# Attention in rounds of two key steps, and eight staging buffers ahead of it

## The reference, cut to what matters

```python
qkv = x @ w_qkv                      # q, k, v; 16 heads; q1, q2 and k1, k2 are halves of a head
a1 = softmax(q1 @ k1.T * scale)      # 1024 x 1024 for every batch and head
a2 = softmax(q2 @ k2.T * scale)
out = (a1 - lam * a2) @ v
out_n = out / rms(out) * norm_w * (1.0 - LAMBDA_INIT)
x = x + reshape(out_n) @ wo          # the reshape mixes heads and rows
x = x + bitlinear(relu(bitlinear(layernorm(x)) + gate * low_rank) ** 2)
```

## Time and profile before

| | |
|---|---|
| time, median of 3 runs | 4335.0 us (4332.88 to 4342.35) |
| time of the profiled execution | 4334.89 us |
| its span | 4333.2 us |
| mean granted TensorE clock | 0.986 |
| busy: PE, DVE, ACT | 4148.5, 3193.5, 2870.7 us |
| first projection matmul | 31.7 us after the start |
| first score of pair 0 | 152.9 us after the start |
| last value products | 3097.9 us |

### The profile page before, as it was taken

The page is one execution under the profiler, slowest core; times in us unless marked ns, Lnnn a source line. Parts: engine busy times, 40 slices in busy tenths (PEclk is TensorE's granted clock), DMA queues, the critical chain, the costliest instruction groups (busy, mean ns, idle before and its releaser), DMA issues.

```text
span 4333.2 us, 57624 instructions
## 1 busy us (share of the span) xinstructions
PE 4148.5 (96%) x22152; PEld 2097.1 (48%) x22152; DVE 3193.5 (74%) x3014; ACT 2870.7 (66%) x3572; POOL 2.0 (0%) x14
## 2 busy tenths in 40 slices
PE   5799999999999999999999999999769999999999
PEld 4333333333333333333333333333257777777777
DVE  4688888888888888888888888899664555555554
ACT  2588878878887887888788788899643333333333
POOL 0000000000000000000000000000000000000000
PEclk9899999999999999999999999999879999999999
DMA  4534433434443443343344334433020101101010
GB/s 159 129 94 97 93 98 90 115 84 94 99 94 96 93 113 83 93 102 93 94 93 114 83 83 108 102 68 68 23 71 20 39 20 39 33 27 39 20 39 20
DMA packets 225843, 338.25 MB, mean 78 GB/s; under 512 B 86704, under 2 KB 107184, under 8 KB 225008
## 3 DMA queue, kind: packets, MB, share of 16 engines
q1 hardware_dynamic: 225520, 333.88, 31.9%
HBM read 180.72 MB, written 150.99 MB: 77 GB/s over the span
## 4 chain that ended last, share of the span: by engine, by line
PE 89%; DVE 3%; DMA 3%; ACT 2%; issue 1%; SPq 1%; DVEq 0%; ACTq 0%
PE ps L534 22%; PE ps L509 19%; PE ps L607 10%; PE ps L622 10%; PE ps L448 9%; PE ps L588 5%; PE ps L451 5%; PE ps L555 3%; PE ps L571 2%; PE ps L612 1%; PE ps L647 1%; DVE fo L1351 1%; PE ps L424 1%; ACT pr L818 1%; PE ps L579 1%
## 5 line engine op out<-in xcount | busy, mean ns | idle before, releaser
L818 ACT ACTIVATE pr<-ps 128x1024 f32<-128x1024 f32 x2048 | 2087.8, 1027 | 556.2 <-PE ps L509 547.3
L1110 DVE TENSOR_TENSOR acc<-acc,pr 128x2048 f32<-128x2048 f32 x768 | 1758.4, 2290 | 111.0 <-ACT pr L818 82.8
L534 PE MATMUL ps<-pr,vst 128*32 128x512 f32 x8192 | 1092.1, 605 | 0.0
L509 PE MATMUL ps<-qst,kst 50*128 50x512 f32 x4096 | 1006.4, 492 | 31.9 <-ACT pr L818 17.9
L509 PEld LDWEIGHTS ps<-qst,kst 50*128 50x128 f32 x4096 | 381.7, 183 | 1296.0 <-issue 980.8
L1110 DVE TENSOR_TENSOR acc<-pr 128x2048 f32<-128x2048 f32 x128 | 293.4, 2293 | 330.1 <-ACT pr L818 330.0
L963 ACT ACTIVATE rb<-ps,scf 128x512 f32<-128x512 f32 x256 | 175.9, 687 | 427.8 <-PE ps L612 427.7
L622 PE MATMUL ps<-tP,hh_ 128*128 128x512 f32 x1024 | 402.9, 393 | 25.4 <-DVE fo L1351 23.5
L607 PE MATMUL ps<-yh,tT 128*128 128x512 f32 x1024 | 410.1, 400 | 0.0
L1316 DVE TENSOR_TENSOR sb<-rb 128x512 f32<-128x512 f32 x256 | 177.1, 692 | 315.1 <-ACT rb L963 313.9
L607 PE MATMUL ps<-yl,tT 128*128 128x512 f32 x1024 | 405.0, 396 | 0.0
(11 more groups left out here) (151 smaller groups left out, 3547.3 us busy)
## 6 DMA issues: line engine op xcount, KB each, us to landing
q_scratch<-stg SPq DMA_DIRECT2D x192, 256.0 KB
k_scratch<-stg SPq DMA_DIRECT2D x192, 256.0 KB
qst<-q_scratch SPq DMA_DIRECT2D x128, 384.0 KB, 6.3
kst<-k_scratch SPq DMA_DIRECT2D x128, 384.0 KB, 9.6
xin<-in_L_attn_x_dram SPq DMA_DIRECT2D x16, 1024.0 KB, 9.6
v_scratch<-vsg SPq DMA_DIRECT2D x64, 256.0 KB, 5.4
vst<-v_scratch SPq DMA_DIRECT2D x128, 128.0 KB, 8.3
xr<-in_L_attn_x_dram SPq DMA_DIRECT2D x64, 256.0 KB
```

Of the source, the lines that this page charges most:

```text
L509: ins = e.matmul(ps[:, 2 * c + hh, :], kst[rows, r, j, t * 128:(t + 1) * 128], qst[rows, r, j, c * 512:(c + 1) * 512], start=True, stop=True)
L534: ins = e.matmul(ps[32 * c4:32 * c4 + 32, 4 + j, :], vst[:, r, t, 32 * hh:32 * hh + 32], pr[:, sl, c, hh, :], start=(t == 0), stop=(t == 7 ...
L818: e.activation(pr[:, sl, c, :, :], ps[:, 2 * c:2 * c + 2, :], ACT.Exp, scale=SCALE).then_inc(s_exp, 1)
L1110: e.tensor_tensor(acc[:, j, :], old, new, ALU.add).then_inc(s_add, 1)
```

## The change

The pair loop goes in eight rounds `d` of two slots, `k` = 2d and 2d + 1; of the posts, `d` 3 is the rms product, 7 the transposes, 14 and 15 the output product. TensorE's order in a round is: value products of slots `k - 3` and `k - 2` in a row (with a sum between them in rounds 1 and 5), score half 1 of slot `k` and half 0 of `k + 1`, all whole-array work of the round, then half 1 of `k + 1` and half 0 of `k + 2`. The first score of the next pair is so issued at the end of round 7 of the pair before. ACT and DVE have new lists, by round and half. Transposes of posts and chunks go to bank 4, the rms matmuls to bank 5, and the flag to 7. The layer norm moves to pairs with `P % 4 == 0`. The second half of the v load moves to round 7, ahead of the shift. In the prologue q and k tiles use eight buffers (`stp`, in space that `pr` takes later), and the conversion of `wo` moves behind tile 20 (its low part behind the tiles).

```diff
-RING, NPB, LAG = 2, 4, 2
+RING, NPB = 2, 4
-PIECES = {1: (0, 4), 2: (0, 4), 4: (0, 4), 7: (1, 2), 8: (1, 2), 9: (1, 4), 10: (1, 4),
-          12: (2, 4), 13: (2, 2), 14: (2, 4), 15: (2, 2)}
+PIECES = {0: (0, 0, 6), 1: (0, 6, 12), 2: (1, 0, 8), 3: (1, 8, 12), 4: (2, 0, 6), 5: (2, 6, 12)}
+STG = 8
+            stp = sbuf(al, "stp", [128, STG, 2, 512], FR)
+        def stage(Q):
+            return stp[:, Q % STG] if Q < 16 else stg[:, Q % 2]
```

Per pair on SP:

```diff
+                for d in range(8):
+                    if d == 0 and P + 1 < NPAIR:
                         sync_load_qk(e, P + 1)
+                    if d in (2, 4, 6) and more:
+                        sync_store(e, 3 * P + 24 + d // 2 - 1)
+                    if d in (2, 7) and P + 1 < NPAIR:
+                        sync_load_v(e, P + 1, d // 7)
+                    if d == 7 and P + 1 < NPAIR:
                         sync_shift(e, P + 1)
+                    if d == 7 and P % 4 == 3 and w + 4 < NC:
+                        sync_x(e, w + 4)
```

Per pair on TensorE:

```diff
+                for d in range(8):
+                    k, gg = 2 * d, 16 * P + 2 * d
+                    if gg >= 4:
+                        pe_pv(e, gg - 3)
+                    if d == 1 and P:
+                        pe_sum(e, P - 1, 1)
+                    if d == 5:
+                        pe_sum(e, P, 0)
+                    if gg >= 2:
+                        pe_pv(e, gg - 2)
                     pe_score(e, P, k, 1)
+                    pe_score(e, P, k + 1, 0)
+                    if d in PIECES and 3 * P + 24 < 24 * B:
...
+                        pe_tile(e, T, 6, n0, n1)
...
+                    if d == 6 and w + 3 < NC:
+                        e.wait_ge(s_pt, 2 * P + 1)
+                        pe_turn(e, w + 3, P % 4, 4)
+                    pe_posts(e, P, d)
+                    if d == 6 and P + 1 < NPAIR:
                         pe_shift(e, flag, P + 1)
+                    pe_score(e, P, k + 1, 1)
+                    if gg + 2 < NSLOT:
+                        pe_score(e, (gg + 2) // 16, (gg + 2) % 16, 0)
```

Per pair on ACT:

```diff
+                for d in range(8):
+                    k = 2 * d
                     act_exp(e, P, k, 0)
+                    if d == 5:
                         act_sum_ln(e, P, 0)
+                        act_sum_exp(e, P, 0)
+                    if P % 4 == 0 and d == 3 and w + 3 < NC:
+                        act_ln(e, w + 3, mv, ln_t, rs)
+                    act_posts(e, P, d, 0)
                     act_exp(e, P, k, 1)
+                    act_exp(e, P, k + 1, 0)
+                    if d in (1, 3, 5) and more:
+                        act_tile(e, 24 + 3 * P + d // 2, 6)
+                    if d == 6 and w + 3 < NC:
+                        act_turn(e, w + 3, P % 4, 4)
+                    act_posts(e, P, d, 1)
+                    act_exp(e, P, k + 1, 1)
```

Per pair on DVE:

```diff
+            steps = {(1, 1): (0, 1), (2, 0): (2, 3), (2, 1): (4,), (3, 1): (6,), (4, 0): (7, 8, 9), (4, 1): (10,)}
+                for d in range(8):
+                    for half in range(2):
+                        if d == 6 and half == 1 and w + 3 < NC:
+                            dve_turn(e, w + 3, P % 4, 4)
+                        if d == 5 and half == 0:
+                            dve_sum(e, P)
+                        dve_posts(e, P, d, half)
+                        if d in (1, 3, 5) and half == 1 and more:
+                            dve_low(e, 24 + 3 * P + d // 2, 6)
+                        if (d, half) in ((2, 1), (4, 0), (6, 0)) and more:
+                            dve_bound(e, 24 + 3 * P + d // 2 - 1)
+                        if P % 4 == 0 and w + 3 < NC:
+                            for n in steps.get((d, half), ()):
+                                dve_ln_step(e, w + 3, n)
+                        dve_add(e, P, 2 * d + half)
...
+                        if P + 1 < NPAIR and (d, half) == (6, 0):
+                            dve_shift(e, flag, P + 1)
```

More of the change, by code:

```diff
@@ L161, in build @@
         s_w = [sem(f"s_w{k}") for k in range(4)]
+        s_stp = [sem(f"s_stp{k}") for k in range(STG)]
         s_stg = [sem(f"s_stg{k}") for k in range(2)]
@@ L526, in pe_pv @@
                     e.wait_ge(s_xtl, 12)
[L527 to L530, removed]
+                if j == 0:
+                    e.wait_ge(s_xtl, min(12 + P, 4 * NC))
+                    if P >= 2:
+                        e.wait_ge(s_otl, P - 1)
+                elif P:
+                    e.wait_ge(s_rmln, P)
             for hh in range(2):
@@ L580, in pe_post @@
                 t.then_inc(s_tr, 1)
-            if 37 <= k < 41:
-                if k == 37:
+            if d in (14, 15):
+                if d == 14:
                     e.wait_ge(s_otl, X + 1)
-                    e.wait_ge(s_rln, min(2 * X + 6, 2 * NPAIR))
+                    e.wait_ge(s_rln, min(2 * X + 5, 2 * NPAIR))
                     e.wait_ge(s_wol, 1)
[L586 to L590, removed]
+                    if X:
+                        e.wait_ge(s_x2v, X)
+                for kk in range(2 * d - 28, 2 * d - 26):
+                    for i, (o_, w_) in enumerate(((oth, woh), (oth, wol), (otl, woh))):
+                        t = e.matmul(ps[:, 7, :], o_[:, kk, :], w_[:, kk, :], start=(kk == 0 and i == 0),
+                                     stop=(kk == 3 and i == 2))
+                if d == 15:
@@ L815, in act_exp @@
                     e.wait_ge(s_add, n_add(f // 16, (f // 8) % 2, f % 8))
[L816 to L817 removed]
+                else:
+                    for Q in range(2 * gg, 2 * gg + 2):
+                        stored(e, 8 + Q)
+                        e.wait_ge(s_qx, 8 + Q + 1)
             e.activation(pr[:, sl, c, :, :], ps[:, 2 * c:2 * c + 2, :], ACT.Exp, scale=SCALE).then_inc(s_exp, 1)
@@ L932, in scalar_program @@
                 act_magnitudes(e, i)
-            for k in range(48):
+            for d in range(24):
                 for half in range(2):
-                    act_posts(e, NPAIR + k // 16, k % 16, half)
+                    act_posts(e, NPAIR + d // 8, d % 8, half)
             e.wait_ge(s_x2, 16 * NPAIR)
@@ L1115, in dve_post @@
             p = X % NP
-            if k == 5:
+            if d == 1 and half == 0:
                 e.wait_ge(s_rex, 2 * X + 2)
@@ L1125, in dve_post @@
                 e.tensor_tensor(ot[:], ot[:], rl[:, 0, :], ALU.add).then_inc(s_ot, 1)
-            if k == 18:
+            if d == 4 and half == 1:
                 e.wait_ge(s_rmex, X + 1)
@@ L1263, in vector_program @@
+            for d in range(24):
+                for half in range(2):
+                    dve_posts(e, NPAIR + d // 8, d % 8, half)
             e.wait_ge(s_x2, 16 * NPAIR)
```

257 lines of the change are left out of this document (94 added, 163 removed).

## The result

The changed kernel takes 4142.0 us (median of 4 runs, 4139.6 to 4162.3) against 4335.2: a ratio of 0.956, 95% interval 0.954 to 0.959. The forecast was 4110, the range 4048 to 4225.

A forecast was written before the change was run, and what follows sets the result against it. TensorE's own instruction order was taken to bound the kernel. Gains of 270 (pairs 3 to 55), 5 (first three) and 25 (prologue), less 44 (layer norms), 14 (batch ends) and 17 (last eight), net 225: 4335 to 4110 us, range 4048 to 4225.

The forecast's parts named there:

- TensorE in the new order: Pair loop: score twos at 0.66, value runs and fewer whole-array runs make a pair 41.7 us against 47.3.
- Rival 2: Pair loop: two in a row cost like two alone, saving just 1.1 us a pair; 4220 to 4290; chance 0.06.
- The rule that the Trainium skill states: Score twos: weight loads overlap only across differing row groups, so about 100 us slower, 4210; shares 0.06 chance.
- ACT keeps up: Rounds with six projection matmuls: exponentials finish 0.1 us before the fourth score needs them; cost 0.
- DVE: Layer norm pairs: DVE needs about 45.3 us, gather about 2.6 late, +3.7 a pair, 44 us in all; ordinary pairs 0.
- The shift row: Next pair's first score, now at the end of round 7, waits 0 to 1.3 us for it; 0.5 taken.
- The batch ends: In 7 pairs the v load waits for a v store landing after 5.4; about 2 us more, 14 in all.
- Rival 3: Shift row lands after 9.6 us, so the first score waits 7.7 in each of 63 pairs; 4500; chance 0.08.
- The last eight pairs: Without projection, rounds take 4.8 us awaiting exponentials: 40.6 a pair against 38.47, 17 us more in all.
- The prologue: Eight buffers spare copies waits for q stores: first score near 128 us, 25 us gained, bounds 8 and 34.
- Pairs 0 to 2: First three pairs, already 42.8 to 44.3 us before: 5 us gained.

The follow-up runs named there:

- experiment 3: Changed kernel with the second value product of a round moved between the first two scores; 4200.2 us (ratio 0.968).
- experiment 2: Changed kernel with the second value product of a round moved behind the first two scores; 4296.9 us (ratio 0.991).
- experiment 1: Changed kernel with two staging buffers in the prologue instead of eight, same loop; 4157.3 us (ratio 0.958).
- Experiment 4: Changed kernel with the shift row's gate raised ahead of slot 11's add and issued in round 6 ahead of the second v load; 4111.1 us (ratio 0.948).
- 6: Changed kernel with ACT's logarithm of the variance in round 4 instead of 3 and DVE's later steps moved back; 4127.3 us (ratio 0.952).
- 7: Changed kernel with early shift row, late logarithm of the variance, and unread filler matmuls in the last eight pairs; 4071.2 us (ratio 0.939).
- 10: Changed kernel with early shift, late logarithm, unread matmuls in the last eight pairs, and v tiles before q and k in even chunks; 4056.5 us (ratio 0.936).
- Experiment 5: Changed kernel with six unread whole-array matmuls in each of five rounds of the last eight pairs; 4108.0 us (ratio 0.947).

## Why the prediction was right, and where it was short

**TensorE in the new order** was right, term by term: 0.66, 1.86, 41.7 forecast and 41.8 to 41.9 found in pairs without a wait. Rival 2 is out: two scores in a row are as cheap in the loop, and taking them apart, with a value run more, costs 0.30 us a round (experiment 3). The second score half still adds 0.24 (0.66 for two, 0.42 for one). The rule that the Trainium skill states in "TensorE: Matmul & The Clock Gate", section "Part 3: Packing small matmuls", by which a pair would have been 43.5 (an estimate), does not hold for these.

**ACT keeps up** was right with the 0.1 us to spare that it claimed, and experiment 2 shows how thin that cover is: with one value product less ahead of a score, six of eight rounds wait.

**DVE** was right as to place: the gather is late by 2.5 us (2.6), and with the avoidable waits gone a pair takes 45.05 (45.3), though DVE idles 2.2 us of it. The term was mis-sized, -44 us forecast and -81 found, but not in its waits. The forecast has 3.7 us of waits for a layer norm pair, and 0.5 for the shift in it and in the next, 4.7 in all; TensorE stood still for 4.3 and 0.5, 4.8 in all, in the mean of the twelve. Its parts are near too: 1.7 for the exponentials (2.1), 2.6 for the shift (2.1), though the latter is 0 to 5.4 by the pair and 1.6 in the same loop of experiment 1, so its mean was hit in part by luck. What the term lacked is the clock. In these two pairs together TensorE ran at 1.2 GHz for 3.7 us, where before it did not at all, and there things take nearly twice the time (two value products in pair 21 stand from 1048.85 to 1052.13, 3.28 us for 1.86). So this is about 1.8 us more, 22 over the twelve (an estimate). The rest of the difference is that the term was put beside ordinary pairs that were charged 0.5 each for the shift. Experiment 4 takes back 31 us, 6 takes 15, and 7 with 10 show the rest as DVE's work.

**The shift row** was charged 0.5 us in each pair and cost nothing in ordinary ones (+10 in the sum: 280 for 270). The batch ends were charged 14 us and cost nothing: v stores now land after a median of 3.2 us, not 5.4. Rival 3 failed: landings of the shift have a median of 2.1 us (2.4 before), 5.7 at most. The lateness that it feared came in layer norm pairs and the ones after them, and otherwise twice in the loop (0.5 and 1.8 us).

**The last eight pairs** were mis-sized, -17 forecast for the eight and -49 found in seven of them. The 4.8 us a round held at full clock: rounds in them begin at 2702.14 and 2706.96. But the granted clock fell behind such rounds, in which TensorE stood still twice for 0.4 to 0.9 us, and the prediction carried rows at full clock into a stretch to which it had just added idle time. Experiment 5 shows it, with pair 59 of experiment 4: 40.65 us at full clock, filled or not. Of the 49 us, about 7 are this run's bad luck (44.51 a pair in experiment 1).

**The prologue** was right (24 for 25); two thirds is the buffers. **Pairs 0 to 2** were forecast 5 us shorter and came out 2 longer; TensorE ran at 1.2 GHz for 18 us in them and for 7 before, which is most of it (about 5.5 us, an estimate).

The misses do not all lie on one side. In the profiled run the forecast was 53 us too good (172 for 225), and by the median 32 (193). Layer norms (37), last pairs (32) and pairs 0 to 2 (7) fell short; the shift (10) and the batch ends (14) were charged and cost nothing, and that these made up for a third of it is luck. Most of what fell short is one thing, some 60 of 77 us by the estimates above: where waits were added, the clock was assumed to stay.

## What to carry to other kernels

Each time TensorE went over to another tile shape and back, it cost about 0.2 us for a run on the whole array or of scores and 0.13 for one of value products with their 32 columns. These are estimates from the rows; experiment 3 measured 0.30 for one of each. So sort an in-order queue by shape, and check for each moved consumer, to 0.1 us, when its exponential ends. When the bound engine gets faster, look at every pair in which the next engine (DVE here) has extra work, and put that work beside the lightest neighbour. And price a stretch where TensorE will idle at the slower clock too; filling it with unread matmuls can pay, as it did here. Last, take the noise of a pair's time from two profiles of the same loop before you read an edit from it.

## What the runs showed of the hardware

TensorE's granted clock fell in the last pairs although it stood still there in pieces of under 1 us only. Pair 58 took 42.28 us at a mean granted clock of 0.96, pair 59 47.24 at 0.86; with the idle pieces filled (experiment 5) two such pairs took 40.66 and 40.67 at 1.00, and pair 59 of experiment 4, not filled, took 40.65 at 1.00. So the same instructions with the same idle pieces ran at either clock from pair to pair. The kernel before was at 1.00 in these pairs. And the small transfers of 8 KB each landed 5.7 us after their issue at worst, against 3.6 before. The worst is 4.6 in experiment 1, with the same order on SP, and 4.9 in experiment 4, with the v load no longer ahead of them; so that load is not shown to be the reason.
